# Edge loops of a two-layer graph network: TensorE's semaphore signals moved from matmuls to drains

## The reference

```python
# layer 0
Q, K, V = x @ WQ, x @ WK, x @ WV          # 8 heads of 16
Eh = edge_attr @ WE
score = exp(clip((K[src] * Q[dst] / sqrt(dh) * Eh).sum(-1), -5, 5))
wV = segment_sum(V[src] * score, dst);  Z = segment_sum(score, dst)
h = x + wV / (Z + 1e-6)                    # then batch norm
...
# layer 1
xl = x @ W
e = leaky_relu(a_src[src] + a_dst[dst], 0.2)
m = segment_max(e, dst)
e = exp(e - m[dst]);  denom = segment_sum(e, dst)
out = segment_sum(e / denom[dst] * xl[src], dst) + bias
# then two linear layers with batch norm and relu
```

## Time and profile before

| | us |
|---|---|
| median of 3 runs | 4707.78 |
| lowest and highest | 4704.26, 4708.37 |
| span of the profiled execution, first to last instruction | 4693.0 |
| TensorE busy (matmuls) | 3812.3 |
| VectorE busy | 3158.1 |
| GpSimd busy | 3369.7 |
| ScalarE busy | 1078.1 |

### The profile page before, as it was taken

One profiled execution on the slowest core, in us unless ns is written; L12 is line 12 of the kernel. 1 busy time (PEld: TensorE's weight loads), 2 busy tenths in 40 slices (PEclk: granted clock), 3 DMA queues, 4 the chain that ended last, 5 costly groups with the idle time before them and its releaser, 6 DMA issues. The chain is left out here.

```text
span 4693.0 us, 76906 instructions
## 1 busy us (share of the span) xinstructions
PE 3812.3 (81%) x19332; PEld 3161.6 (67%) x19333; DVE 3158.1 (67%) x8279; ACT 1078.1 (23%) x4010; POOL 3369.7 (72%) x3437
## 2 busy tenths in 40 slices
PE   6889899989989988888898977777777777777778
PEld 5777777777778877767567755655555556555555
DVE  1877677677777776777646866666666666666657
ACT  3100010000000000000034433333333333333324
POOL 3677777777777777777557777777777777777752
PEclk9887787787776787888687555555555555555559
DMA  7666665666666666666424322222222222222224
GB/s 279 182 182 184 176 189 176 179 183 181 183 181 182 182 183 174 185 179 183 148 86 97 61 61 61 61 61 61 61 61 61 61 61 60 60 61 61 61 58 154
DMA packets 376029, 593.47 MB, mean 126 GB/s; under 512 B 151298, under 2 KB 204520, under 8 KB 374488
## 3 DMA queue, kind: packets, MB, share of 16 engines
q0 software_dynamic: 132880, 330.18, 27.4%
q1 hardware_dynamic: 241544, 255.24, 18.2%
q10 hardware_dynamic: 1552, 7.43, 0.4%
HBM read 551.16 MB, written 40.54 MB: 126 GB/s over the span
## 5 line engine op out<-in xcount | busy, mean ns | idle before, releaser
L393 POOL DMA_INDIRECT kv_g<-kv_table,idx x1661 | 1678.2, 1010 | 568.0 <-issue 498.7
L1065 POOL DMA_INDIRECT xg<-xl_table,idx x1661 | 1583.0, 953 | 519.3 <-issue 498.6
L1130 PEld LDWEIGHTS ps_sum<-pw,xg 128*128 128x128 f32 x3328 | 740.9, 328 | 165.9 <-DVE pws L1271 165.5
L1130 PE MATMUL ps_sum<-pw,xg 128*128 128x64 f32 x3328 | 819.1, 428 | 4.7 <-DVE pws L1271 2.2
L452 PE MATMUL ps_sum<-kv_g,hot 128*64 128x136 f32 x3328 | 606.6, 339 | 246.8 <-issue 245.8
L1117 PE MATMUL ps_tops<-ident,top 128*64 128x128 f32 x832 | 285.9, 447 | 518.7 <-DVE top L1243 518.4
L452 PEld LDWEIGHTS ps_sum<-kv_g,hot 128*64 128x64 f32 x3328 | 480.9, 167 | 314.9 <-issue 310.2
L438 PE MATMUL ps_pair<-w,eat 128*128 128x128 f32 x3328 | 616.3, 342 | 5.1 <-issue 5.1
L438 PEld LDWEIGHTS ps_pair<-w,eat 128*128 128x128 f32 x3328 | 524.2, 240 | 109.3 <-issue 71.7
L442 PE MATMUL ps_pair<-qw,hott 64*128 64x128 f32 x3328 | 583.9, 326 | 2.9 <-DMA qw<-q_table 2.9
L1229 DVE SCALAR_TENSOR_TENSOR ps_lg<-raw 128x256 f32<-128x256 f32 x416 | 185.3, 445 | 573.4 <-ACT raw L1178 566.7
(11 more groups left out here) (160 smaller groups left out, 4684.9 us busy)
## 6 DMA issues: line engine op xcount, KB each, us to landing
eat<-in_edges SPq DMA_DIRECT2D x416, 256.0 KB
local<-local_table SPq DMA_DIRECT2D x416, 128.0 KB, 3.8
kv_g<-kv_table,idx POOLq DMA_INDIRECT x1661
xg<-xl_table,idx POOLq DMA_INDIRECT x1661
qw<-q_table SPq DMA_DIRECT2D x416, 32.0 KB
adw<-ad_row SPq DMA_DIRECT2D x416, 32.0 KB, 5.1
kv_table<-kv_out SPq DMA_DIRECT2D x25, 512.0 KB, 2.6
xl_table<-xl SPq DMA_DIRECT2D x25, 264.0 KB, 2.8
```

The source lines that it names most:

```text
L393: nc.gpsimd.indirect_dma_start(out=kv[:, u, k, 0:2 * D], out_offset=None, in_=m["kv_table"], in_offset=bass.IndirectOffsetOnAxis(ap=idx[:, ...
L1065: nc.gpsimd.indirect_dma_start(out=xg[:, u, k], out_offset=None, in_=m["xl_table"], in_offset=bass.IndirectOffsetOnAxis(ap=idx[:, u // B, ...
L1130: nc.tensor.matmul(ps_sum[:, b, 0:W], xg[:, u, k, 0:D], pw[:, b, k], start=(k == 0), stop=(k == K - 1))
```

## The change

In both edge loops each signal of TensorE to the other engines is raised by a drain, an instruction of its own behind the last matmul of the group. In loop 1 these are `summed` behind L452 and `turned` behind L461 (and behind L442 for the first two chunks); in loop 2 `turned` behind L1117 and `summed` behind L1131 (and one `turned` behind the last L1121). Matmuls, operands, waits, buffers and the order of the steps are the same. That makes two drains per chunk in each loop, 4 x 416 in all, and three at the ends.

```diff
--- before.py
+++ after.py
@@ -439,9 +439,9 @@
                 pe.wait_ge(window_in[u % 4], landed(c, u % 4, 16, 4))
                 pe.wait_ge(hott_ready, c + 1)
                 for k in range(K):
-                    mm = nc.tensor.matmul(ps_q[:, b, k], hott[:, b, at(k, P)], qw[:, u % 4], start=True, stop=True)
+                    nc.tensor.matmul(ps_q[:, b, k], hott[:, b, at(k, P)], qw[:, u % 4], start=True, stop=True)
                 if first:
-                    mm.then_inc(turned, 1)
+                    nc.tensor.drain().then_inc(turned, 1)
 
             def sum_up(c, u):
                 b = u % 2
@@ -449,17 +449,17 @@
                 pe.wait_ge(valued, c + 1)
                 pe.wait_ge(sums_out, c - 1 + LEAD)
                 for k in range(K):
-                    mm = nc.tensor.matmul(ps_sum[0:W, b, 0:D + H], hot[:, u % 4, k], kv[:, u, k, D:ROW0],
-                                          start=(k == 0), stop=(k == K - 1))
-                mm.then_inc(summed, 1)
+                    nc.tensor.matmul(ps_sum[0:W, b, 0:D + H], hot[:, u % 4, k], kv[:, u, k, D:ROW0],
+                                     start=(k == 0), stop=(k == K - 1))
+                nc.tensor.drain().then_inc(summed, 1)
 
             def turn_sums(c, u):
                 b = u % 2
                 pe.wait_ge(sums_out, c + 1 + LEAD)
                 pe.wait_ge(added, c - 1 + LEAD)
                 nc.tensor.matmul(ps_turn[:, b, 0:W], sums[:, b, 0:D], m["ident"][0:W, 0:W], start=True, stop=True)
-                nc.tensor.matmul(ps_turn[0:H, b, W:2 * W], sums[:, b, D:D + H], m["ident"][0:W, 0:W],
-                                 start=True, stop=True).then_inc(turned, 1)
+                nc.tensor.matmul(ps_turn[0:H, b, W:2 * W], sums[:, b, D:D + H], m["ident"][0:W, 0:W], start=True, stop=True)
+                nc.tensor.drain().then_inc(turned, 1)
 
             spread_out(0, 0, True)
             spread_out(1, 1, True)
@@ -1114,21 +1114,23 @@
             pe.wait_ge(row_kept, NG)
             def turn_top(c, u):
                 pe.wait_ge(largest, c + 1)
-                nc.tensor.matmul(ps_top[0:W, u % 2, 0:P], top[:, u % 2], m["ident"][:], start=True, stop=True).then_inc(turned, 1)
+                nc.tensor.matmul(ps_top[0:W, u % 2, 0:P], top[:, u % 2], m["ident"][:], start=True, stop=True)
+                nc.tensor.drain().then_inc(turned, 1)
 
             def spread_max(c, u):
                 pe.wait_ge(column, c + 1)
-                mm = nc.tensor.matmul(ps_max[:, u % 2, 0:W], col[:, u % 2:u % 2 + 1].to_broadcast([W, P]),
-                                      m["ident"][0:W, 0:W], start=True, stop=True)
+                nc.tensor.matmul(ps_max[:, u % 2, 0:W], col[:, u % 2:u % 2 + 1].to_broadcast([W, P]),
+                                 m["ident"][0:W, 0:W], start=True, stop=True)
                 if isinstance(c, int) and c == NC - 1:
-                    mm.then_inc(turned, 1)
+                    nc.tensor.drain().then_inc(turned, 1)
 
             def sum_up(c, u):
                 b = u % 2
                 pe.wait_ge(slots_summed, c + 1)
                 for k in range(K):
                     nc.tensor.matmul(ps_sum[:, b, 0:W], xg[:, u, k, 0:D], pw[:, b, k], start=(k == 0), stop=(k == K - 1))
-                nc.tensor.matmul(ps_sum[:, b, W:2 * W], ones, pws[:, b], start=True, stop=True).then_inc(summed, 1)
+                nc.tensor.matmul(ps_sum[:, b, W:2 * W], ones, pws[:, b], start=True, stop=True)
+                nc.tensor.drain().then_inc(summed, 1)
 
             for c in range(3):
                 turn_top(c, c)
```

## The result

| | before | after |
|---|---|---|
| median of 4 runs each, us | 4706.02 | 4735.62 |
| lowest and highest, us | 4702.68, 4708.37 | 4731.32, 4757.86 |
| span of the profiled execution, us | 4693.0 | 4732.2 |

The ratio of the two is 1.0075, with a 95% interval of 1.005 to 1.0099: the changed kernel is slower by some 24 to 47 us. The prediction said 4714 with a range of 4702 to 4765, so the time lies in the range, 22 us above the likeliest value; "slower by over 0.2%", which came, had a chance of 0.41 in it. What made the time was not in the sum, though, but in a rival; the part on the prediction takes this up.

A forecast was written before the change was run, and what follows sets the result against it. GpSimd's gathers were taken to bound both loops, hiding most drain time; 3.0 + 1.0 + 0.5 + 1.2 + 0.8 = +6.5 us on the median 4707.78 gave 4714, with a range of 4702 to 4765.

The forecast's parts named there:

- rival C: Loop 1: GpSimd's gathers run beside VectorE instructions less or more often; 25 us faster or slower, chance 0.05 each.
- Price of a drain, 0.3 us: TensorE, both loops: 0.08 us of lost overlap plus 0.21 us for starting a new group, per drain.
- The cover in loop 1: TensorE's chunk grows from 4.72 to 5.15 us at a low-clock share of 0.42, still under GpSimd's 5.27.
- 3 us for full buffers: Loop 1: allowance of 3 us for times when the eight buffers fill and GpSimd stands still.
- Start of loop 1: The gather that waits for the second chunk's sums comes later: +1.0 us.
- Start of loop 2: The gather that waits for the first sums, behind four turns of the prologue, comes later: +0.5 us.
- End of loop 1: After the last gather two to three chunks run out at TensorE's pace: +1.2 us.
- End of loop 2: After the last gather four chunks of sum, add and slot sum, each signalled later: +0.8 us.
- Rival A: TensorE becomes the bound of loop 1 past 0.35 us a drain: +37 us at 0.4, +122 at 0.5; chance 0.11.
- Rival B: TensorE's clock stays low in loop 1: +800 us, 5510, or 4790 in the mild form; chance 0.05.
- Rival D: Drains cost nothing measurable, hidden in TensorE's existing waits: 4708; forecast's chance 0.68, with this case 0.74.
- Carrying over the 14.8 us: The runs' median lay 14.8 us above the profiled span; this was kept, giving 4707.78 + 6.5 = 4714.3.

The follow-up runs named there:

- e9: Kernel before, without drains, with VectorE's L555 and L576 in loop 1 each reading one operand from PSUM: 4598.15 us, 0.9783 of the kernel before.
- e10: Changed kernel, all drains, with VectorE's L555 and L576 each reading one operand from PSUM: 4598.59 us, 0.9774 of the kernel before.
- e12: Changed kernel with two more drains per chunk of loop 1, behind L438's and L442's groups: 4784.45 us, 1.0186 of the kernel before.
- e3: Kernel before with a drain only behind the sums of loop 1 (`summed`): 4772.0 us, 1.0157 of the kernel before.
- e2: Kernel before with the drains of loop 2 only: 4702.4 us, 1.0004 of the kernel before.
- e5: On a slower chip, kernel before without drains, L555 and L576 each reading one operand from PSUM: 5715.0 us, 1.0061 of the kernel before there.

## Why the prediction was right, and where it fell short

The number is right by the width of the range and not by the sum. The sum's terms were to make +6.5 us and made none of the time; the time came by rival C's slower form, which had a chance of 0.05 and for whose sake, with A's, the range went up to 4765. Rival C's own figure, 4714 + 25 = 4739, is 3 us from the 4735.6 measured. By the sign that the prediction set for itself, "gathers of another mean than 1010 ns (C)", its main line was wrong: the mean is 1031.

- **GpSimd as the bound of both loops**: right. Take 108 us out of its instructions and the kernel is 104 us faster (e9).
- **Price of a drain, 0.3 us**: right at low clock, from 7.19 us (median 7.28) for 7.23 with two, 6.92 and 6.91 with one (0.28 each); at full clock a median of 4.26 us for 4.26. In loop 2 it was half of it: 3.85 - 3.56 = 0.29 for two.
- **The cover in loop 1**: right, with more room than worked out. The step "at that share" held the share of low-clock time at 0.42; it fell to (1 - 0.83)/0.5 = 0.34, which gives TensorE 1/(0.34/7.23 + 0.66/4.26) = 4.95 us per chunk, not 5.15. In e10 it is (1 - 0.86)/0.5 = 0.28. The share is a result of the loop, not a constant of it.
- **3 us for full buffers**: wrong in sign; the waits for `summed` in loop 1 changed by -3.0 us. **Start of loop 1** +1.0: the longest wait went from 20.9 to 21.2. **Start of loop 2** +0.5: 7.66 for 7.39 us. **End of loop 1** +1.2: -1.9, since more of it ran at full clock, the uncertainty that the text named. **End of loop 2** +0.8: +0.2. Together these terms made -4.4 where +6.5 stood. The first later gather of loop 2, forecast near 2538, came at 2560.5, shifted by loop 1.
- **Rival A**: not here, the waits stayed below 29.1 us; e12 shows it from about 5.28 us per chunk. **Rival B**: not here, the clock rose; e3 shows its mild form at 0.75. **Rival D**, no cost, holds in loop 2 (e2), and to within some 10 us in loop 1 as soon as nothing meets (e10).
- **Rival C is what happened**, on its slower side. Its cause is right: 64 ns of the gathers' mean lie in such instructions as the one beside L576, and all 65 ns are gone in e9. The step that failed is "the meetings spread over all phases", on which it was priced at 25 us to either side and left out of the sum at a chance of 0.05 each way. They don't spread: of 92 long gathers at low clock in before 65 have the next one five gathers later, and by the account above they repeat where three or five gathers with a meeting last as long as a chunk. The term measured +34.7 us in loop 1 in the two traces. Rows that stood there gave reason to doubt that step, though not the sign: the full-clock chunk was to go from 3.91 to 4.26 us, close to the 4.16 of three gathers with a meeting of 1.36, but the low-clock chunk was to leave 6.63, close to five gathers with one (6.66), for 7.23.
- **Carrying over the 14.8 us** between span and median was wrong by itself: the profiled execution of after took 4734.0 us for a span of 4732.2, so 1.8 lie outside the span, and the profiled execution of before, by the same 1.8, was 11 to 13 us faster than the medians of its kind. Runs of before spread from 4686 to 4716 us over two chips. So of the 39.2 us between the spans about 10 are chance, and the medians differ by 29.6; every difference above that is taken between two traces carries such a doubt.

## What to carry to other kernels

When an edit lengthens a step on an engine that isn't the bound, ask not only whether the cover holds but what the new spacing does to the bound engine: compare a whole number of its instructions, with and without one disturbed, with the new length of the loop step. Where the bound engine's instructions have a mean above their median, find what runs beside the long ones first; here giving two VectorE instructions an operand in PSUM was worth 2.2%. And leave a signal on the matmul where there is no reason for a drain: the drain is free at best, and on the chip where the gathers gave no cover the two loops' drains cost 5.4%.

## What the hardware showed beyond that

- Behind a drain the next matmul starts 0.21 to 0.36 us after the end of the last, at either clock, in the rows shown (before L452 at full clock, 0.25 stood there without one); a chunk grows by 0.28 us per drain at 1.2 GHz in loop 1 and by 0.15 in loop 2.
- TensorE's mean clock in loop 1 rose with drains in both places (0.79, 0.83, and 0.89 with four), and fell with one behind the sums (0.75).
- A gather instruction of 0.95 us takes 1.35 to 1.8 us when it begins between 0.34 us ahead of and 0.14 us behind the start of a TENSOR_TENSOR of 128x512 with two SBUF inputs: it then ends 1.49 to 1.51 us behind that start. With one of these inputs in PSUM it takes 0.95. A TENSOR_SCALAR of 64x512 is itself lengthened by a gather, from 0.47 to as much as 0.72 us.
- The kernel before took 21% longer on one chip (5683.46 for 4702.12 us), with instructions of the same length; e5 there has twice the idle time before loop 1's gathers that e9 has (1166.7 for 567.5).
